# A four-layer graph network in one kernel: the second attention score by DMA, the aggregation and the final rows at other places of the half step

## The reference

```python
# layer 3, graph attention
h = x @ W;  s1 = h @ a1;  s2 = h @ a2
e = leaky_relu(s1[:, :, None] + s2[:, None, :], 0.2) * mask
att = softmax(e, axis=2)
x_out = elu(att @ h + beta * h)
# layer 4, gated recurrence, 3 steps; in_mat = out_mat = adj
a_in = a_out = adj @ h;  av = concat(a_in, a_out)
z  = sigmoid(w3(av) + u3(h));  r = sigmoid(w4(av) + u3(h))
hv = tanh(w5(av) + u5(r * h));  h = (1 - z) * h + z * hv
```

## Time and profile before

| | |
|---|---|
| median of three runs | 1502.7 us |
| the profiled execution | 1503.36 us |
| its span, first to last instruction | 1501.6 us |
| mean granted TensorE clock | 0.991 |
| busy: PE, DVE, ACT, POOL | 1464.4, 1244.5, 990.1, 538.7 us |
| second stage | from about 606 us to the end |
| one group of six halves | 111.90 us |

### The profile page before, as it was taken

One profiled execution on the slowest core, in us unless ns is written; L12 is line 12 of the kernel. 1 busy time (PEld: TensorE's weight loads), 2 busy tenths in 40 slices (PEclk: granted clock), 3 DMA queues, 4 the chain that ended last, 5 costly groups with the idle time before them and its releaser, 6 DMA issues.

```text
span 1501.6 us, 45862 instructions
## 1 busy us (share of the span) xinstructions
PE 1464.4 (98%) x18922; PEld 1237.2 (82%) x18922; DVE 1244.5 (83%) x2517; ACT 990.1 (66%) x1795; POOL 538.7 (36%) x623
## 2 busy tenths in 40 slices
PE   8999999899999997799999999999999999999997
PEld 7898999899888886688888788887887887887886
DVE  4888877989999998888888888888888888888767
ACT  5767767667777776666666666666666666666564
POOL 3876776767888885411101101111111111111000
PEclk9999999999999999899999999999999999999999
DMA  8300000002333234100000000000000000000000
GB/s 267 87 2 0 0 0 2 16 17 45 65 68 65 56 58 59 29 1 1 29 1 2 30 1 1 30 1 1 30 1 1 30 1 1 29 2 1 29 2 28
DMA packets 36839, 40.89 MB, mean 27 GB/s; under 512 B 11872, under 2 KB 31840, under 8 KB 36704
## 3 DMA queue, kind: packets, MB, share of 16 engines
q0 software_dynamic: 4608, 16.78, 5.9%
q1 hardware_dynamic: 32096, 22.10, 4.9%
HBM read 13.71 MB, written 8.39 MB: 15 GB/s over the span
## 4 chain that ended last, share of the span: by engine, by line
PE 91%; DVE 5%; ACT 1%; POOL 1%; issue 1%; DMA 0%; DVEq 0%; POOLq 0%
PE ring L99 43%; PE scores L99 28%; PE scores L1706 3%; PE ring L1506 3%; PE scores L1470 3%; PE ring L1546 2%; PE ring L1775 2%; PE ring L1517 2%; PE ring L1690 1%; PE ring L1847 1%; PE ring L1648 1%; PE ring L1659 1%; PE ring L1671 1%; DVE s L1035 1%; PE ring L1679 0%
## 5 line engine op out<-in xcount | busy, mean ns | idle before, releaser
L543 POOL TENSOR_TENSOR s<-s,mx 128x512 f32<-128x512 f32 x128 | 138.2, 1103 | 56.8 <-DVE mx L1040 56.8
L617 POOL TENSOR_TENSOR r_var_eps<-r_mean_var,eps 128x4 f32<-128x4 f32 x16 | 8.1, 508 | 377.1 <-DVE r_mean_var L1208 377.1
L549 POOL TENSOR_TENSOR s<-s,rtotal 128x512 f32<-128x512 f32 x128 | 130.8, 1059 | 31.6 <-DVE rtotal L1046 31.4
L701 ACT ACTIVATE s<-s 128x512 f32<-128x512 f32 x128 | 77.9, 642 | 69.0 <-POOL s L543 68.8
L1371 DVE TENSOR_TENSOR rhp_lo<-r,rhp_hi 128x1024 fp32r<-128x1024 f32 x47 | 57.6, 1225 | 73.4 <-ACT rhp_hi L916 73.4
L1035 DVE SCALAR_TENSOR_TENSOR s<-scores,mask 128x512 f32<-128x512 f32 x128 | 87.1, 681 | 30.6 <-PE scores L1470 30.6
L881 ACT ACTIVATE r<-r,bias_half 128x512 f32<-128x512 f32 x96 | 64.3, 717 | 58.9 <-DVE r L1342 58.9
L935 ACT ACTIVATE hv<-scores,bias 128x512 f32<-128x512 f32 x94 | 64.7, 689 | 55.0 <-PE scores L99 55.0
L909 ACT ACTIVATE later_w<-ring 128x512 f32<-128x512 f32 x64 | 34.8, 596 | 99.0 <-PE ring L1775 99.0
L713 ACT ACTIVATE pT<-ring 128x512 f32<-128x512 f32 x128 | 66.1, 603 | 42.4 <-PE ring L1506 42.4
L1040 DVE TENSOR_REDUCE mx<-s 128x8 f32<-128x512 f32 x128 | 87.9, 686 | 4.4
(11 more groups left out here) (314 smaller groups left out, 5129.8 us busy)
## 6 DMA issues: line engine op xcount, KB each, us to landing
x<-beta_less_one POOLq DMA_DIRECT2D x16, 512.0 KB, 4.7
x<-o POOLq DMA_DIRECT2D x16, 512.0 KB, 6.6
out_x<-x SPq DMA_DIRECT2D x15, 512.0 KB, 2.9
x<-in_x SPq DMA_DIRECT2D x1, 6144.0 KB, 25.4
later_w<-in_L_gnn_w_w SPq DMA_DIRECT2D x3, 512.0 KB, 6.4
x<-in_x SPq DMA_DIRECT2D x2, 512.0 KB, 5.3
x<-in_x SPq DMA_DIRECT2D x1, 1024.0 KB, 7.4
stage<-in_L_gnn_w_qkv SPq DMA_DIRECT2D x3, 256.0 KB, 3.1
```

Source lines behind the costliest of these rows:

```text
L543: pool.tensor_tensor(sr, sr, mx[:, r, :].unsqueeze(2).to_broadcast([P, CT * 2, N]), ALU.subtract).then_inc(s_shifted, 1)
L549: pool.tensor_tensor(sr, sr, rtotal[:, r, :].unsqueeze(2).to_broadcast([P, CT * 2, N]), ALU.mult).then_inc(p_ready, 1)
L701: act.activation(s[:, par, r, :, :, :], s[:, par, r, :, :, :], ACT.Exp).then_inc(p_exp, 1)
```

## The change

1. `graph_s2` on PE goes for chunks 2 to 15 (it stays for 0 and 1). SP takes its place: two DMAs write column 257 of `hw` (4 bytes an element, 256 elements each) to DRAM, and after both have landed two more read it back, the same 256 numbers to each of 64 partitions, into `e`. DVE then adds the first score in place in one operation on 128 partitions instead of two on 64.
2. Layer 3 of a chunk now takes three halves: a (k = 1, 3), s (k = 2, 4) and b (k = 3, 5). Half s holds the scores, the exponential and the softmax, and ends with `graph_attT` behind `w5`. Half b copies `attT` on DVE and has `graph_aggregate` directly behind the adjacency products. PE's second half of `u3` in half b waits for that copy, since it writes the bank of `attT`.
3. PE's `w4` stands before all `graph_product`s, `w3` before 2 and 3 of them. ACT copies all four tiles of `hw` behind the tanh of r.
4. ACT copies `hu` earlier and between the two tanh of z.
5. The transposes of a chunk's final rows stand at the end of the half (behind `w5`), and DVE adds them to `x` in the next half, behind `r*h`.
6. SP's program alternates the stores of finished chunks with the spreads.

The core of the diff:

```diff
+                def spread_s2(c):
+                    sp.wait_ge(hw_copied, (c + 1) * FT)
+                    for g in range(2):
+                        sp.dma_start(rows[g, :].rearrange("(t j) -> j t", t=CT), hw[g * N:(g + 1) * N, :, D + 1])\
+                            .then_inc(s2_gathered, 16)
+                    sp.wait_ge(s2_gathered, 32 * (c - 1))
+                    for g in range(2):
+                        sp.dma_start(e[g * N:(g + 1) * N, :, :].rearrange("p t j -> p (t j)"), spread_rows(rows[g, :], N))\
+                            .then_inc(s2_spread, 16)
...
# ACT
                     for m in range(FT):
+                        act.wait_ge(hu_ready, n * FT + m + 1)
+                        act.activation(hu[:, m, :], ring[:, 2 + m, :], ACT.Copy).then_inc(hu_copied, 1)
                         act.wait_ge(z_added, (n - 1) * FT + m + 1)
...
+                    if s.graph_b is not None:
+                        graph_read(s.graph_b, ring, s.y_bank)
...
-                    if s.graph_a is not None:
-                        copy_hw(s.graph_a, 0)
-                        copy_hw(s.graph_a, 1)
...
+                    r_tanh(n)
                     if s.graph_a is not None:
-                        copy_hw(s.graph_a, 2)
-                        copy_hw(s.graph_a, 3)
+                        for t in range(CT):
+                            copy_hw(s.graph_a, t)
# DVE
+                def graph_scores_spread(c):
+                    dve.wait_ge(hw_copied, (c + 1) * FT)
+                    dve.wait_ge(s2_spread, 32 * (c - 1))
+                    dve.tensor_tensor(e[:], e[:], hw[:, :, D:D + 1].to_broadcast([P, CT, N]), ALU.add).then_inc(e_sum, 1)
+                    graph_rectified(c)
# PE
+                            if m == 1 and s.graph_b is not None:
+                                pe.wait_ge(attT_copied, s.graph_b + 1)
                             product(pe, ring[:, 2 + m, :], columns(wT["u3"], m), moving(hp[s.me])).then_inc(hu_ready, 1)
...
                         adjacency(r_hn[s.me] if s.step == 0 else tok)
+                    if s.graph_b is not None:
+                        if s.y_bank == 2:
+                            wait_apart(pe, hu_copied, n * FT)
+                        graph_aggregate(s.graph_b, ring, s.y_bank)
...
+                    for m in range(FT):
+                        product(pe, ring[:, m, :], columns(wT["w4"], m), moving(agg)).then_inc(r_ready, 1)
...
                         graph_product(s.graph_a, 0)
                         graph_product(s.graph_a, 1)
...
+                    for m in range(FT):
+                        product(pe, high[:, m, :], columns(wT["w3"], m), moving(agg)).then_inc(z_ready, 1)
                     if s.graph_a is not None:
                         pe.wait_ge(hw_copied, s.graph_a * FT + 1)
                         graph_product(s.graph_a, 2)
                         graph_product(s.graph_a, 3)
-                    if s.graph_b is not None:
-                        graph_aggregate(s.graph_b)
-                    if s.graph_a is not None:
-                        graph_s2(s.graph_a)
...
+                    if s.graph_s is not None:
+                        pe.wait_ge(hu_copied, n * FT)
+                        graph_attT(s.graph_s, ring, 3)
+                    if s.leaves is not None:
+                        pe.wait_ge(h_done, n * FT)
+                        pe.wait_ge(r_added, (n + 1) * FT)
+                        final_rows(s, 0)
```

More of the change, by code:

```diff
@@ L115, in load_columns, with network @@
     return ap.rearrange("(f p) -> p f", p=P)
[L118 removed]
+def network(nc, x, ident, psum, layers, a, out, s2_rows):
     scores, ring = psum
@@ L421, in __init__ @@
                         self.leaves = group * 2 - 1
-                self.left = group * 2 - 2 if self.k == 0 and not self.first else None
-                self.left_before = group * 2 - 1 if self.k == 1 and not (fixed and group == 0) else None
+                self.left = None
+                if self.k == 0 and not self.first:
+                    self.left = group * 2 - 2
+                if self.k == 1 and not (fixed and group == 0):
+                    self.left = group * 2 - 1
                 self.later = group * (HALVES - 2) + self.k
@@ L433, in __init__ @@
                 self.stats = {3: even, 5: odd}.get(self.k) if goes_on else None
-                self.norm = {4: even, 5: odd}.get(self.k) if goes_on else None
-                self.after_a = {2: even, 4: odd}.get(self.k) if goes_on else None
-                self.after_b = {3: even, 5: odd}.get(self.k) if goes_on else None
+                self.norm = {4: even}.get(self.k) if goes_on else None
+                if self.k == 0 and not self.first and not self.last:
+                    self.norm = group * 2 + 1
             def h_before(self):
@@ L1387, in half @@
                     if s.graph_b is not None:
-                        copy_attT(s.graph_b)
+                        graph_negative(s.graph_b)
                     update(s, 1)
-                    if s.enters is not None:
+                    if s.enters is not None and s.k != 0:
                         enter(s.enters, s.other)
-                    if not s.last:
-                        r_sum(n)
+                    r_sum(n)
+                    if s.enters is not None and s.k == 0:
+                        enter(s.enters, s.other)
                     if s.before_step < STEPS - 1:
@@ L1400, in half @@
                         close_rh(s)
-                    if not s.last:
-                        z_sum(n)
-                    if s.graph_a is not None:
[L1404 to L1408, removed]
+                    if s.graph_s is not None:
+                        graph_attention(s.graph_s)
+                    if s.k == 3 and s.stats is not None:
+                        recurrence_stats(s.stats)
+                    z_sum(n)
+                    if s.k == 5 and s.stats is not None:
+                        recurrence_stats(s.stats)
+                    if s.closing:
+                        leave(s.leaves, ring, 2)
                 x_stats(0, 0)
@@ L1800, in half @@
                                 pe.wait_ge(r_added, n * FT)
+                            if s.left is not None:
+                                pe.wait_ge(left, (s.left + 1) * 2)
                             graph_rows(s.graph_a)
@@ L1921, in build @@
                       beta=a["L1_gnn_ln_beta"])
-        network(nc, x, ident, (scores, ring), (first, second), a, out)
+        network(nc, x, ident, (scores, ring), (first, second), a, out, s2_rows)
 INPUTS = ["x", "adj", "L0_gnn_Wq", "L0_gnn_bq", "L0_gnn_Wk", "L0_gnn_bk", "L0_gnn_Wv", "L0_gnn_bv",
```

161 lines of the change are left out of this document (87 added, 74 removed).

## The result

| | before | after |
|---|---|---|
| median of the runs | 1502.7 us | 1604.2 us |
| span of the profiled execution | 1501.6 | 1602.2 |
| mean granted TensorE clock | 0.991 | 0.971 |

The change makes the kernel slower: ratio 1.0686, 95% interval 1.067 to 1.0703. The forecast was 1512.1 with a range up to 1527; the sign was right, the size was not.

A forecast was written before the change was run, and what follows sets the result against it. The prediction took PE, busy all of a 111.9 us group, as the bound. Waits of 3.34 less 2.0 saved a group added 9.4 us over 7 groups to 1503.36, less 0.7 for the median: 1512.1 us, range 1496 to 1527.

The forecast's parts named there:

- The transfers: Gather to DRAM and read back before DVE's addition into `e`: hidden by 1.3 us, cost 0.
- the lower end, 7.7: Shortest estimate in us for the chain of gather, read back and issues, taken because the DMA queue is quiet.
- The cover of 9.0: Time from the end of the `hw` copies until DVE needs `e` in half s: 9.0 us.
- upper end of 13.1: Longest estimate for the transfer chain, landings of 5.7 us each plus 1.7 of issues: 13.1 us.
- The rival with the right mechanism: Spread lands late, PE waits for `att` in halves s: 14 us per microsecond over cover, up to 1569; chance 0.10.
- the clock does not fall for waits this short: PE's products after its waits run at full pace, as after 2.3 us of idle; 0.10 lost per product wait.
- PE's saving: Spread 0.80 and aggregation's lengthening of the next product 0.20 a chunk: 2.0 a group, 14.0 us in all.
- The waits in the new order: Six places of a group where PE waits for ACT or DVE: 3.34 us a group.
- For `hw`: PE's `graph_product` 2 waits for ACT's copies: 0.81 us in k = 1, 0.69 in k = 3.
- For the attention: PE's transposes of `att` at the end of k = 2 and 4 wait 0.38 us each time.
- For the copy of `attT`: u3's second half in k = 3 and 5 waits 0.34 us for DVE's copy, plus 0.10 lost.
- The sum of the order: Waits of 3.34 against 2.0 saved: 1.34 us longer a group, 9.4 us over 7 groups.

The follow-up runs named there:

- e1: The changed kernel without the second scores' DMA gather and read back, adjacency values standing in for them in DVE's addition: 1521.3 us.
- e4: The changed kernel with ACT first copying each partition's four second scores side by side, so the gather writes 128 pieces of 16 bytes: 1524.5 us.
- e2: The kernel before with the 14 spreads of later chunks left out of PE, adjacency values standing in, nothing moved: 1495.2 us.
- e6: The 16-byte version (1524.5 us) with ACT's copies of the first two `hw` rows put ahead of the tanh of r: 1511.6 us.
- e3: The changed kernel with one gather over 128 partitions instead of two over 64, and a strided DVE addition: 1583.4 us.
- e10: The 16-byte version, scores side by side in SBUF but written 4 bytes at a time to DRAM, read back as in the change: 1593.1 us.

## Why the prediction was wrong

**The transfers: the step that failed.** "So I take the lower end, 7.7: hidden by 1.3 us, cost 0." The cover of 9.0 was right (8.96 in e1). The chain was 13.0, at the upper end of 13.1, and there for another reason than the upper end had: the gather took 8.3 where I had put 3.0 to 5.7, while the read back at 3.5 lay near the lower landing and the issues took 1.1 (0.62 and 0.49) rather than 1.7. The row that I called nearest, 256 elements of 4 bytes at 5.7, I put down to the large transfers ahead of it; no run tells whether that was so. For the gather it was the pieces: with 16 bytes in place of 4 (e4) the whole change is 1524.5 us. By the page's rule on strided last dimensions, which the prediction had put beside the sum (the Trainium skill, DMA: Bandwidth & Descriptors, Rules for kernel authors), each element is a descriptor of its own, and the traces agree: packets under 512 bytes rise by 8064 from before to after (11872 to 19936), 576 a chunk, and fall by 384 a chunk with 128 pieces in place of 512 (14561 in e4). The fixed part of about 2 us, which I had cited beside it from the same page's section on the anatomy of one DMA, does not contain what the pieces cost: the gather alone took 8.3.

**The rival with the right mechanism had the price too low.** "Each microsecond over it costs 14": 4.0 us over the cover cost 59 us of PE's waits (70.0 − 10.7), close to 14 × 4.0. Its 1569 lacks 35 us: 9.2 of the order's own (1521.3 for 1512.1), 2.3 of waits (59.3 for 57), and 23.6 that are no wait of PE (82.9 − 59.3). Of these 22.3 are the lower clock behind a wait of 4.7 us: the stretch from the transposes of `att` to the first piece behind u3 is 85.4 us over the 14 places in after and 63.1 in e1, where the clock stays up. The step "the clock does not fall for waits this short" was true of the 0.4 to 0.8 us that it spoke of, and I never priced it for the rival.

**PE's saving** was priced rightly and not gained in full. Of the 14.0 forecast, 11.2 were the spreads: rows give 0.78 each, 11.0 in all, and e2 gains 7.1. The rest went into the gaps at the turn of the loop, 2.5 to 5.4 us by the view of waits. Read from starts, the two halves around the turn take 3.6 us longer than the same halves outside the loop in before, summed over its four turns, and 7.0 in e2: 3.4 us more, which leaves 7.6. I had no term for these gaps. The other 2.8 were the aggregation's. e2 does not test them, but rows do: adjacency, aggregation and the product behind it take 1.09 + 1.02 + 2.91 before and 0.98 + 0.98 + 2.80 in e1, 0.26 less against the 0.20 forecast.

**The waits in the new order** were there, in their places. For `hw`: 0.81 and 0.69 forecast, 9.4 / 14 = 0.67 measured in e1, 12.9 us in all by e6 against 11.9. For the attention: 0.38 forecast, 0.65 measured, and 0.81 by starts (w5 and the wait take 3.61 where w5 alone takes 2.80). One cause is visible: the first gating of `hv` behind the scores takes 0.98 on DVE where the second takes 0.69, in the time in which POOL shifts the scores (after; the last row is POOL's):

```profile
1166.17 0.98 DVE L1360 SCALAR_TENSOR_TENSOR hv<-later_w,hv 128x512 f32<-128x512 f32 x1
...
1168.52 0.69 DVE L1360 SCALAR_TENSOR_TENSOR hv<-later_w,hv 128x512 f32<-128x512 f32 x1
```

```profile
1165.62 0.99 POOL L660 TENSOR_TENSOR e<-e,g_mx 128x256 f32<-128x256 f32 x1 [21.00 <-DVE g_mx L1271]
```

It is 0.98 or 0.99 in all 14 halves s, and 0.69 to 0.72 in the others of this size; that POOL is the cause is argued from this, no run takes it away. The 0.29 is as much as the 0.27 that was missing; I had counted every update at its undisturbed length. For the copy of `attT`: 0.34 and 0.10 forecast. PE's timeline of e1 shows the gap between the halves of u3:

```profile
1165.62 0.39 PE L99 MATMUL ring<-hp_b_hi,u3T_lo 128*128 128x512 f32 x1
1166.07 0.50 PE L99 MATMUL ring<-hp_b_hi,u3T_hi 128*128 128x512 f32 x1
1166.40 0.40 PE L99 MATMUL ring<-hp_b_lo,u3T_hi 128*128 128x512 f32 x1
```

0.45 and 0.33 in place of 0.23 each, so 0.22 and 0.10.

**The sum of the order.** e1 is 18.4 us over the 1502.97 of its own comparison, the forecast had 9.4. Outside the loop's turn a group is 110.9 us before and 112.9 in e1 (six halves, from u3 to u3), so 2.0 a group where the forecast had 1.34, 14 in all; the turns add 3.8 (3.6 to 7.3 by starts). Together that is 17.8. Of the 0.7 missing in a group the attention is 0.86, the waits for `hw` 0.14, the copy of `attT` −0.24 and a saving that is 0.2 larger than forecast −0.2, which makes 0.56. The sign was right for the reason given, the waits outweigh the saving; of the 9.0 us missing 3.8 lie in the gaps at the turn, which had no term. Had the gather been quick, the time would have lain inside the range given (e4 at 1524.5, range to 1527), at its far end.

**The chances.** Slower by over 0.2% had 0.68, rightly. Late transfers had 0.10, with a chain known only to lie between 7.7 and 13.1 and 9.0 of cover: three quarters of that interval lie beyond the cover. The value was taken at the end that costs nothing, and the range was cut at 10 us of chain.

## What to carry to other kernels

Price a small DMA by its pieces, not by its bytes: for 2 KB in 512 pieces of 4 bytes SP waited 7.2 to 8.1 us, in 128 pieces of 16 bytes 1.4, and a copy of 0.21 us on ACT and an addition that is 0.19 longer on DVE make the one into the other. If a cover lies inside the bounds of an unmeasured latency, the forecast does not belong at the near end, and a wait of 4 to 5 us on the bounding engine was paid as idle time (59 us) and again as the slower clock behind it (22 us). Work that leaves the critical engine is worth less than its rows if the instruction stream has gaps near by that grow when it is gone.

## What the runs showed of the hardware

- A gather is slow if either side of it, the read in SBUF (e3) or the write to DRAM (e10), is in 4-byte pieces: 7.2 us of SP's wait each, against 1.4 with both in 16 bytes. 384 more pieces for 5.8 us (e10 against e4) to 6.7 us (after against e4) are 15 to 17 ns for each; this is an estimate from these runs.
- The clock: after 2.3 us of idle PE ran at full pace, after 4.7 us the granted clock was 0.50 for 4.2 us, where transposes and the first products took up to twice as long. Over 14 such places it cost 22.3 us (after against e1).
- A half-size DVE operation (128x512) takes 0.98 rather than 0.69 us when POOL works on a 128x256 tile (1.0 us) beside it, 14 times of 14 in every version of the new order. That POOL is the cause is argued.
- PE's gaps without a releaser at the turn of the loop doubled (4 to 8, 2.5 to 5.4 us) when the 16 small products of each spread were taken out (before against e2).
